# Where GpSimd's list of a step puts its three scatters: after the power, ahead of the next mask

## The reference, cut to what matters

```
xn  = layernorm(x)
q, k, v, g = xn @ Wq, xn @ Wk, xn @ Wv, xn @ Wg        # 4 heads, 32 wide for q and k, 64 for v and g
gk  = log_sigmoid(xn @ Wgk + bgk) / 16                 # decay of each token and head
o   = gated linear attention of q, k, v with decays exp(cumsum(gk)), causal, state carried on
on  = o * rsqrt(mean(o*o, last axis) + 1e-5) * gnorm_w
att = (on * g * sigmoid(g)) @ Wo
e   = argmax(softmax(xn @ gate_w)), p = its probability  # 8 experts
ffn = p * (gelu(xn @ w1[e] + b1[e]) @ w2[e] + b2[e])
out = x + att + ffn
```

## Time and profile before

| what | value |
| --- | --- |
| median of 3 runs | 436.61 us (436.0 to 437.3) |
| profiled execution, its own time | 436.22 us |
| its span, first to last instruction | 434.4 us |
| mean granted TensorE clock | 0.989 of full speed |
| busy: TensorE | 389.0 us (90%) |
| busy: VectorE | 326.3 us (75%) |
| busy: ScalarE | 310.0 us (71%) |
| busy: GpSimd | 297.1 us (68%) |

### The profile page before, as it was taken

How to read it: one execution, slowest core, us unless ns; L and a number is a source line. 1 busy time by engine, 2 the same in 40 slices (tenths; PEclk the granted TensorE clock), 3 DMA queues, 4 the chain that set the end, 5 groups by cost and what they waited for, 6 DMA issues and landing times.

```text
span 434.4 us, 13589 instructions
## 1 busy us (share of the span) xinstructions
PE 389.0 (90%) x3650; PEld 336.6 (77%) x3651; DVE 326.3 (75%) x930; ACT 310.0 (71%) x949; POOL 297.1 (68%) x245
## 2 busy tenths in 40 slices
PE   6866889989989899898998999989999999999990
PEld 5645678877767777676776777879999999999990
DVE  5977798988788778778778777866776876767660
ACT  4769888886877868778678687746666766666660
POOL 7532253357878778788787874328888888888884
PEclk9989999999999999999999999999999999999996
DMA  8726489435445343364453424015554555555530
GB/s 239 200 63 194 143 240 314 139 107 172 147 135 182 96 139 116 127 174 136 149 176 119 147 101 129 26 38 69 68 72 61 68 63 64 70 69 67 68 36 0
DMA packets 59098, 51.30 MB, mean 118 GB/s; under 512 B 7201, under 2 KB 51393, under 8 KB 59073
## 3 DMA queue, kind: packets, MB, share of 16 engines
q1 hardware_dynamic: 45936, 42.07, 33.2%
q0 software_dynamic: 12272, 8.54, 14.1%
q10 hardware_dynamic: 864, 0.40, 0.4%
HBM read 33.14 MB, written 18.30 MB: 118 GB/s over the span
## 4 chain that ended last, share of the span: by engine, by line
PE 52%; DVE 13%; issue 11%; ACT 11%; POOL 8%; DMA 1%; DVEq 1%; ACTq 1%; SPq 0%; POOLq 0%
PE psA L905 15%; PE psVG L893 14%; ACT E L1067 6%; PE psVG L722 5%; PE psA L735 4%; DVE msn L1384 4%; POOL sorted_rows L550 4%; PE psQK L710 3%; POOL rms L544 3%; PE psT L780 3%; PE psO L754 2%; DVE stats L1221 2%; ACT sq L1076 2%; PE psT L788 1%; DMA x_all<-in_L_attn_x_dram 1%
## 5 line engine op out<-in xcount | busy, mean ns | idle before, releaser
L584 POOL DMA_INDIRECT out_dram<-yw,sidx x71 | 115.0, 1619 | 29.1 <-issue 11.3
L550 POOL DMA_INDIRECT sorted_rows<-x_all,pos_i x64 | 73.0, 1140 | 35.3 <-PE psT L780 26.3
L1067 ACT ACTIVATE E<-gcB,ngc 128x128 f32<-128x128 f32 x256 | 78.6, 403 | 0.0
L537 POOL TENSOR_SCALAR_AFFINE_SELECT E<-E 128x1024 f32<-128x1024 f32 x32 | 35.6, 1111 | 41.7 <-ACT E L1067 41.4
L544 POOL TENSOR_TENSOR rms<-msn,neg_half 128x8 f32<-128x8 f32 x32 | 53.3, 1664 | 9.2 <-DVE msn L1384 8.5
L1040 ACT ACTIVATE qb<-psQK,qmask 128x256 f32<-128x256 f32 x64 | 26.9, 474 | 38.7 <-PE psQK L710 35.8
L1412 DVE TENSOR_TENSOR pr<-psA,E 128x512 f32<-128x512 f32 x64 | 41.0, 682 | 16.7 <-POOL E L537 16.6
L754 PEld LDWEIGHTS psO<-v_sb,pr 128*64 128x64 f32 x1024 | 38.2, 137 | 18.3 <-issue 11.6
L754 PE MATMUL psO<-v_sb,pr 128*64 128x64 f32 x1024 | 42.3, 225 | 8.1 <-DVE og L1424 5.4
L905 PE MATMUL psA<-xT_all,v_sb 128*128 x288 | 38.3, 276 | 0.4 <-issue 0.4
L893 PE MATMUL psVG<-xgT,gcB 128*128 128x128 f32 x288 | 38.6, 277 | 0.0
(11 more groups left out here) (191 smaller groups left out, 944.4 us busy)
## 6 DMA issues: line engine op xcount, KB each, us to landing
gcB<-decay_rows SPq DMA_DIRECT2D x32, 512.0 KB
sorted_rows<-blank SPq DMA_DIRECT2D x12, 396.0 KB, 5.3
xg<-sorted_rows SPq DMA_DIRECT2D x71, 66.0 KB
x_all<-in_L_attn_x_dram SPq DMA_DIRECT2D x16, 256.0 KB, 5.4
out_dram<-res SPq DMA_DIRECT2D x32, 128.0 KB
eqB<-decay_exp_rows SPq DMA_DIRECT2D x32, 64.0 KB
w1b<-in_L_ffn_w_dram SPq DMA_DIRECT2D x8, 256.0 KB
xT_all<-in_L_ffn_w_dram SPq DMA_DIRECT2D x32, 64.0 KB
```

Of the source, the lines that this page charges most:

```text
L537: nc.gpsimd.affine_select(out=E[j][:], in_=E[j][:], pattern=[[0, 2 * H], [1, P]], compare_op=ALU.is_ge, fill=0.0, base=0, channel_multipli ...
L550: nc.gpsimd.indirect_dma_start(out=sorted_dram, out_offset=bass.IndirectOffsetOnAxis(ap=pos_i[:, t:t + 1], axis=0), in_=x_all[:, t, :], in ...
L584: nc.gpsimd.indirect_dma_start(out=out_rows, out_offset=bass.IndirectOffsetOnAxis(ap=sidx[j][:], axis=0), in_=yw[j][:], in_offset=None, bo ...
L1067: last = nc.scalar.activation(E[j][:, k, h * P:(h + 1) * P], gcB[j][:, k * H + h, :], ACT.Exp, bias=ngcf[:, bass.ds((s * 2 + k) * H + h, 1)])
```

## The change

GpSimd's list of a step is put in another order; no instruction is added or removed. The mask of the first sequence is done ahead of the loop and each step masks the next sequence at its end. All three scatters of a step stand in a row between the power and that mask. Scatter t+1 now waits for `s_ready` of `state(s)`, and scatter t+2 for `wo_ready` of `project_out(s-2)` where it waited for `oT_ps_ready` of `transpose_on(s-1)`. Scatter t waits for the same `qk_ready` as before.

```diff
--- before.py
+++ after.py
@@ -552,25 +552,26 @@
 
             def step(s):
                 t = (s - PLACE_FROM) * 3
-                if s < SEQS:
-                    mask_dec(*divmod(s, 2))
+                if s >= 1:
+                    if s >= 2:
+                        pool.wait_ge(dve_on, s - 1)
+                    rms_step(*divmod(s - 1, 2))
+                if s == 2:
+                    finish_band()
                 if s == PLACE_FROM:
                     pool.wait_ge(dve_late, LATE)
                     pool.wait_ge(sort_cleared, CLEARS * 16)
                 if s >= PLACE_FROM and t < TILES:
                     pool.wait_ge(qk_ready, s + 2)
                     place_rows(t)
-                if s >= 1:
-                    if s >= 2:
-                        pool.wait_ge(dve_on, s - 1)
-                    rms_step(*divmod(s - 1, 2))
-                if s == 2:
-                    finish_band()
-                if s >= PLACE_FROM and t + 1 < TILES:
+                    pool.wait_ge(s_ready, s + 1)
                     place_rows(t + 1)
-                    pool.wait_ge(oT_ps_ready, s)
+                    pool.wait_ge(wo_ready, s - 1)
                     place_rows(t + 2)
-
+                if s + 1 < SEQS:
+                    mask_dec(*divmod(s + 1, 2))
+
+            mask_dec(0, 0)
             for s in range(SEQS + 1):
                 step(s)
```

## The result

The changed kernel takes 451.1 us (448.6 to 451.3, 4 runs) against 437.0 (436.0 to 437.3, 4 runs): ratio 1.031, 95% interval 1.027 to 1.035. I had forecast 417.7 us, and faster. The profiled execution took 451.25 us, its span is 449.5.

A forecast was written before the change was run, and what follows sets the result against it. Bound: GpSimd and TensorE waiting for each other in a circle, 7.84 us a step. Gains of 1.30, 0.66, 15.96 and 0.96 make 18.9 us, taking the profiled 436.2 to 417.3, median 417.7; range 414.5 to 430.

The forecast's parts named there:

- the circle: In steps with three scatters, GpSimd's mask and TensorE's transposes wait for each other; its links sum to 7.85 us.
- the floor: TensorE's own time for an attention step, 6.88 us, reached if nothing else sets the pace.
- GpSimd's list: GpSimd's mask, power and three scatters with their gaps in one step: 6.94 us, taken as 7.0.
- The two new waits cost 0: At scatters t+1 and t+2: both awaited semaphores are already up, and the old transposes wait with its 0.82 us goes.
- What is left is GpSimd's own list in a row: After the change only GpSimd's instructions in sequence remain to count: 5.27 + 1.27 + 0.40 = 6.94 us.
- g: Gap between a scatter and the scatter before it whose wait is long met; 0.20 us taken, bounds 0.02 to 0.82.
- the three signs: Prediction wrong if row gaps near 0.8 us, if x_lo or `on` exceed 0.42 and 0.69, or mask waits for E.
- preparation not hidden: Slower rival, scatters in a row: a scatter can't be prepared behind another, 8.18 us a step, 440 us; chance 0.09.
- The early hold of the mask on VectorE: Slower rival: the mask's hold catches `on`, delaying `msn` and the power; 10.1 us a step, some 475; chance 0.03.
- Half of it: Rival: VectorE's work beside the row makes scatters dearer, 7.3 to 7.8 us a step; 429 us at 7.6; chance 0.20.
- Step 7: Its wait of 1.23 us for `res` goes; the step falls from 8.19 to 6.89 us and gives 1.30.
- Step 8: Takes 8.21 us with no wait at the transposes; gain between 0 and 1.32 us, taken as 0.66.

The follow-up runs named there:

- two: The changed kernel without the third scatter of a step, 43 of 64 tiles scattered; 415.0 us, ratio 0.950.
- third_half: The changed kernel with only 64 rows in scatter t+2, its other 64 left out; 414.9 us, ratio 0.951.
- first_half: The changed kernel with only 64 rows in scatter t, its other 64 left out; 417.3 us, ratio 0.956.
- half: The changed kernel with scatters of 64 rows instead of 128; 414.9 us, ratio 0.952.
- direct: The changed kernel with plain DMAs of GpSimd's queue in place of the indirect ones, tiles written unsorted; 415.2 us, ratio 0.952.
- old_wait: The changed kernel with scatter t+2 given its former wait for the transposes again; 423.8 us, ratio 0.969.
- spaced: The changed kernel with a memset of 512 columns ahead of scatter t+1 and of scatter t+2; 428.3 us, ratio 0.980.
- mask_second: The changed kernel with the next sequence's mask moved ahead of the second scatter; 428.6 us, ratio 0.983.
- wo_wait: The kernel before the change with only the new wait of scatter t+2; 433.8 us, ratio 0.995.
- short: The changed kernel with a memset of 256 columns between scatters t+1 and t+2; 418.8 us, ratio 0.959.
- mask_third: The changed kernel with the next sequence's mask moved ahead of the third scatter; 418.8 us, ratio 0.959.
- fill_first: The changed kernel with a memset of 256 columns ahead of scatter t+1 only; 446.9 us, ratio 1.024.
- fill_small: The changed kernel with a memset of 128 columns ahead of scatter t+2; 452.2 us, ratio 1.034.

## Why the prediction was wrong

**Right: the circle, and cutting it.** The bound of the kernel before was the circle mask, scatter t, power, `on`, transposes, scatter t+2. In the changed kernel GpSimd's wait for the transposes is gone, and where rows or positions are left out and the stall with them (`two`, `third_half`, `first_half`, `half`, `direct`) the period falls from 7.84 to 6.89 us. In `old_wait`, `spaced`, `mask_second` and `wo_wait`, with 7.21 to 7.73, another wait or a longer list sets the pace.

**Right: the floor.** I took 6.88 us for TensorE. `two`, `half` and `direct` run at 6.89.

**The mechanism right, the size off: GpSimd's list.** I summed it to 6.94 and took 7.0. From `short` and `old_wait`: the power 0.18 behind the mask instead of 0.37, which I took for the gap of two neighbours and which was a wait: the bracket in the earlier trace rows names `msn`; scatter t 1.03 instead of 1.27, the lower bound; a scatter behind a scatter at 0.30 instead of 0.20. Without the memset that is 1.10 + 0.18 + 1.67 + 0.20 + 1.03 + 0.30 + 0.96 + 0.30 + 0.96 + 0.01 = 6.71 us, under TensorE's 6.89. Without the stall the kernel would by my estimate have stood near 415 us, like `third_half` and `direct`, at the lower edge of my range. Scatter t costs 1.03 when it starts ahead of `on`, and 1.50 when `on` starts first: in `mask_third` `on` starts at 207.57, 0.11 us ahead of the scatter at 207.68. The Trainium skill, page "SBUF — State Buffer", practical consequences of the port table, infers that a tensor_tensor with two SBUF inputs does not hold up descriptor generation. These rows do not fit that, with 1.50 us against 0.96 to 0.98; whether the scatter is held while it writes descriptors or while it reads its positions no run here tells.

**The step that failed: "The two new waits cost 0", with "What is left is GpSimd's own list in a row".** The waits themselves cost next to nothing: in `short` and `two`, where there is no stall, no gap ahead of scatters t+1 and t+2 that ends with them is over 0.2 us. In the changed kernel `s_ready` holds scatter t+1 in two steps, with gaps of 0.93 and 1.41 us, because the stall makes `state` late; these are the steps of 1.97 and 2.44 us between the first two scatters. What I costed at nothing is that the old wait kept the scatters apart. Before, scatters start 2.3 to 2.9 us from each other, three of them in 5.0 us at the least: behind a mask, a power, or a wait of 0.82 us. I looked for what the new order would make GpSimd wait for, and priced a row of scatters by GpSimd's time alone (g from 0.02 to 0.82 us). What three of them within 2.8 us do to the other engines' sequencers was in no term; it is about 1.3 us of TensorE's time in a step, and the period is 8.56 us where I had 7.0. The range, 414.5 to 430, was built from bounds of g and of scatter t and so could not hold it. No row of before shows three that close; the earlier trace rows have two, but of 1.55 us each. Nor did any of the three signs that I had named for being wrong appear: the gaps in which GpSimd waits for nothing are 0.30 to 0.55, `on` takes at most 0.68 and `x_lo` 0.42 but for a few of up to 0.49, and the mask does not wait for E.

**How a 1.3 us stall becomes 1.7 us a step.** With the circle cut TensorE is the bound, and a hole of 1.3 us in its list adds in full. `outputs` and ScalarE end late, `sq`, `ms` and `msn` with them, and the power is 1.2 to 1.3 us behind the mask in the steps shown, not 0.18: it is late as an effect, not as the cause. The remaining 0.4 us are not explained.

**The rivals.** The slower rival that I had, preparation not hidden, named the right place, scatters in a row, but the wrong mechanism: g is 0.30, not 0.82. It would have been 440 us. The early hold of the mask on VectorE did not occur: `msn` takes 0.17 us in the changed kernel, where the power waits for it and not for the mask; I had expected it near 1.7. "Half of it" did not occur for its reason either: no second scatter was held up by VectorE's work.

**The single steps.** Step 7 gave its 1.30 (its transposes start 6.89 us after step 6's, not 8.19). Step 8 lost: 10.34 instead of 8.21, the first full stall, where I had taken a gain of 0.66; in `two` it takes 7.22, in `short` 7.74, so a gain of 0.5 to 1.0 us was there without the stall. Steps 9 to 28 lost 0.72 each where I had 0.84 as gain (0.96 for step 28).

**What stays open.** What in the chip stops the sequencers. The runs show what brings it on, three indirect scatters of 96 or 128 rows in 2.5 to 2.9 us, a part of it still in single steps with up to 3.8, and that lists of positions do it where as many bytes do not; SyncE's loads make it about 0.3 us a step worse. What draws the line between 2.79 us in `short`, free of it, and 2.80 in `fill_first`, not free, is only named by the last distance, not explained, and `fill_small` shows that this distance is not the whole condition either. Between 64 and 96 rows nothing was tried.

## What to carry to other kernels

A wait that looks like pure loss may keep apart what must not come close; before removing it, write down how far apart the instructions behind it start now and will start then, and treat a distance that no row of the old trace shows as an unknown with a price on every engine, not only its own. Put needed work between indirect scatters of GpSimd, as the mask here: at the same instruction count `mask_third` gives 418.8 us where the row of three gives 451.1. In a trace, look for idle time "for nothing that the profile shows" between identical instructions and for register moves that take longer than usual: they tell a stopped sequencer from a missing input.

## What the runs showed of the hardware

- Where three indirect DMAs of 96 or 128 rows from GpSimd start within 2.5 to 2.9 us, TensorE stands still for about 1.3 us in most steps of the changed kernel, and ScalarE, GpSimd and SyncE have holes of 0.7 to 0.8 us; in `fill_first` ScalarE and SyncE are hit and TensorE is not. With 1.45 us between the last two in every step (`short`), with two of them, with 64 rows in the first or the last, or with direct DMAs there are none.
- An indirect scatter behind another takes a gap of 0.30 us and 0.96 us (`short`); a direct DMA from the same queue takes 0.54 us (`direct`).
- Beside a tensor_tensor of 128x512 with two inputs in SBUF that has started before it, an indirect scatter takes 1.50 us (`mask_third`, `mask_second`).
- After a true wait an indirect scatter starts 0.82 us behind what it waited for (`old_wait`, `wo_wait`).
- In the changed kernel the stall makes the time vary from step to step: periods from 6.89 to 10.34 us, where those of `short` are 6.92 or 6.93 in steps 9 to 27.
